# Sliding-window attention between two expert layers: one sigmoid per score block, and the blend ahead of the scores

## The reference

```python
x = x + 0.5 * ffn(layernorm(x))      # x W_base^T + b + gated low-rank experts (top 2 of 8)
x = x + attn(layernorm(x))
x = x + 0.5 * ffn(layernorm(x))      # the same weights

def attn(x):                         # H = 32 heads of DH = 128, one K and V for all heads
    Q, K, V = x @ Wq.T, x @ Wk.T, x @ Wv.T
    Qr, Kr = rope(Q), rope(K)
    for i in range(0, S, 256):       # windows of 512, half overlapping
        attn = sigmoid(Qr[i:i+512] @ Kr[i:i+512].T * SCALE)
        attn = attn / attn.sum(-1)
        wout = attn @ V[i:i+512]
        # first half: out = (1 - alpha) * out + alpha * wout; second half: out = wout
    return out @ Wo.T
```

## Time and profile before

| | |
|---|---|
| median of 3 executions | 4590.61 us (4590.13 to 4811.48) |
| the profiled execution, its own time | 4577.35 us |
| its span, slowest core (5) | 4575.8 us |
| spans of the eight cores | 4546.6 to 4575.8 us |
| mean granted TensorE clock of the cores | 0.826 to 0.832 |
| busy: TensorE, ScalarE, VectorE, GpSimd | 69%, 28%, 22%, 12% of the span |

### The profile page before, as it was taken

How to read it: one execution, slowest core, us unless ns; L and a number is a source line. 1 busy time by engine, 2 the same in 40 slices (tenths; PEclk the granted TensorE clock), 3 DMA queues, 4 the chain that set the end, 5 groups by cost and what they waited for, 6 DMA issues and landing times.

```text
span 4575.8 us, 40221 instructions; the slowest of 8 cores (4546.6 to 4575.8 us)
## 1 busy us (share of the span) xinstructions
PE 3136.4 (69%) x14804; PEld 1492.0 (33%) x14804; DVE 995.1 (22%) x1698; ACT 1303.2 (28%) x1727; POOL 533.3 (12%) x772
## 2 busy tenths in 40 slices
PE   2449999994366666666666666666676665349999
PEld 1224444442223332233332233322333321224444
DVE  3441111115612220012210023200122100441111
ACT  3332211214422322232322332223323232332222
POOL 1101111111111111200002100012000022101111
PEclk8669999996688777887778887778887787669999
DMA  5325565554453436831127711067411178427776
GB/s 126 97 58 166 169 178 171 171 152 119 124 150 111 124 97 117 145 88 37 56 44 143 145 37 46 28 112 141 97 37 50 36 140 155 110 79 209 221 223 188
DMA packets 647220, 537.35 MB, mean 117 GB/s; under 512 B 33905, under 2 KB 566642, under 8 KB 646770
## 3 DMA queue, kind: packets, MB, share of 16 engines
q0 software_dynamic: 90112, 251.71, 23.8%
q1 hardware_dynamic: 556914, 283.07, 23.3%
HBM read 408.85 MB, written 125.83 MB: 117 GB/s over the span
## 4 chain that ended last, share of the span: by engine, by line
PE 53%; DMA 18%; DVE 11%; ACT 10%; issue 5%; DVEq 1%; SPq 0%; ACTq 0%; POOL 0%; POOLq 0%
PE PS L441 24%; PE PS L754 7%; PE PS L602 7%; DMA x2h<-arena 6%; DMA arena<-wqT 4%; DMA arena<-woT 4%; PE PS L688 4%; ACT arena L273 4%; ACT arena L668 2%; PE PS L673 2%; DVE arena L248 2%; DVE arena L252 2%; DVE arena L695 2%; DVE arena L706 2%; PE PS L651 2%
## 5 line engine op out<-in xcount | busy, mean ns | idle before, releaser
L441 PE MATMUL PS<-arena 128*128 128x512 bf16 x5120 | 1135.7, 380 | 15.5 <-ACT arena L273 15.5
L273 ACT ACTIVATE arena<-arena 128x512 bf16<-128x512 f32 (+1 forms) x784 | 567.4, 762 | 1052.8 <-PE PS L444 578.3
L754 PE MATMUL PS<-arena 128*128 128x512 bf16 x2048 | 594.7, 456 | 348.9 <-ACT arena L273 348.9
L441 PEld LDWEIGHTS PS<-arena 128*128 128x128 bf16 x5120 | 501.9, 98 | 623.3 <-issue 22.3
L602 PE MATMUL PS<-arena 128*128 128x512 bf16 x2048 | 584.9, 428 | 19.7 <-ACT arena L273 19.6
L754 PEld LDWEIGHTS PS<-arena 128*128 128x128 bf16 x2048 | 222.8, 113 | 720.0 <-issue 582.9
L45 POOL DMA_DIRECT2D x2h<-arena x256 | 217.2, 849 | 1943.3 <-ACT arena L762 1683.7
L762 ACT ACTIVATE arena<-PS 128x512 f32<-128x512 f32 x256 | 152.8, 597 | 662.5 <-PE PS L754 448.9
L695 DVE COPY arena<-PS 128x516 f32<-128x516 f32 (+1 forms) x160 | 94.2, 589 | 1044.2 <-PE PS L688 1044.2
L602 PEld LDWEIGHTS PS<-arena 128*128 128x128 bf16 x2048 | 215.3, 108 | 264.7 <-issue 104.8
L448 DVE TENSOR_SCALAR arena<-arena 128x512 f32<-128x512 f32 x160 | 77.1, 482 | 823.2 <-DMA arena<-xin 464.6
(11 more groups left out here) (102 smaller groups left out, 2270.9 us busy)
## 6 DMA issues: line engine op xcount, KB each, us to landing
arena<-wbaseT SPq DMA_DIRECT2D x256, 512.0 KB, 6.7
x2h<-arena POOLq DMA_DIRECT2D x320, 256.0 KB, 4.7
arena<-wqT SPq DMA_DIRECT2D x256, 256.0 KB, 3.4
arena<-woT SPq DMA_DIRECT2D x256, 256.0 KB, 5.5
arena<-xin POOLq DMA_DIRECT2D x24, 1024.0 KB, 11.5
arena<-xin POOLq DMA_DIRECT2D x96, 256.0 KB, 5.3
x1h<-arena POOLq DMA_DIRECT2D x96, 256.0 KB, 2.4
arena<-x1h POOLq DMA_DIRECT2D x24, 1024.0 KB, 9.6
```

The costliest lines, as they stand in the source:

```text
L273: c = pr.emit("scalar", lambda s, si=i % nb, d=dst_bf_ap: s.activation(d, wstage[si], ACT.Copy), wc, 1)
L441: pr.emit("tensor", lambda t, c=c, sl=slot, of=of, t0=t0, n=n: t.matmul(sl, wb[of % 2][:, c, :], xlnb[:, c, t0:t0 + n], start=(c == 0), st ...
L754: mmc = pr.emit("tensor", lambda t, gg=gg, of=of, ts2=ts2, sl=slot: t.matmul(sl[:, 0:512], wqb[of % 2][:, gg, :], wout8[:, gg, ts2 * 512:( ...
```

## The change

In each window the blend, where one is pending, now comes first. Then each of the four key blocks has a matmul and a sigmoid of its own: blocks 0 and 2 in the first half of PS2, blocks 1 and 3 in the second. The matmul of block 2 waits for the sigmoid of block 0, that of block 3 for the sigmoid of block 1, and the first one for rope and the last sigmoid of the window before. `feed(6)` stands behind block 1 and behind block 3, `feed(4)` behind the matmuls with V as before; these wait for the sigmoid of block 3.

In `ln_prep` the index `par` of the float buffers `xf` and of their semaphores is renamed `xpar` (it is `i % 2` as before), the list of two buffers is written as a comprehension, and two semaphores `xload4` and `xload5` are declared. A list `sig_kc` is set up ahead of the heads. The rest of the diff:

```diff
@@ -637,12 +640,6 @@
                     npp = qn // 128
                     kc0 = wi * 2
                     sp = wi % 2
-                    w01 = [("vector", rope[h]), ("scalar", sig2_prev)]
-                    for kc in (0, 1):
-                        s01 = pr.emit("tensor", lambda t, kc=kc, q0w=q0w, qn=qn, kc0=kc0, par=par: t.matmul(
-                            PS2[:, kc * 512:kc * 512 + qn], krb[:, (kc0 + kc) * 128:(kc0 + kc + 1) * 128],
-                            qrb[par][:, q0w:q0w + qn], start=True, stop=True),
-                            w01 if kc == 0 else [], 1 if kc == 1 else 0)
                     if pend_blend is not None:
                         b, sA, wpar, dgc, hh_ = pend_blend
                         pend_blend = None
@@ -659,27 +656,31 @@
                         woutev = pr.emit("scalar", lambda s, hh_=hh_, b=b: s.activation(
                             wout8[:, hh_, b * 256:(b + 1) * 256], PS4[:, 0:256], ACT.Copy),
                             [("tensor", tw), ("tensor", womm_prev_grp)], 1)
+                    sgw = []
+                    if (h, wi - 2) in av_hist:
+                        sgw = [("tensor", av_hist[(h, wi - 2)])]
+                    elif wi < 2 and h >= 1:
+                        sgw = [("tensor", av_hist[(h - 1, 4 - wi)])]
+                    for kc in range(4):
+                        wsc = []
+                        if kc == 0:
+                            wsc = [("vector", rope[h]), ("scalar", sig_cnt)]
+                        elif kc >= 2:
+                            wsc = [("scalar", sig_kc[kc - 2])]
+                        smm = pr.emit("tensor", lambda t, kc=kc, q0w=q0w, qn=qn, kc0=kc0, par=par: t.matmul(
+                            PS2[:, (kc % 2) * 512:(kc % 2) * 512 + qn],
+                            krb[:, (kc0 + kc) * 128:(kc0 + kc + 1) * 128],
+                            qrb[par][:, q0w:q0w + qn], start=True, stop=True), wsc, 1)
+                        sig_kc[kc] = pr.emit("scalar", lambda s, qn=qn, sp=sp, kc=kc: s.activation(
+                            sgb[sp][:, kc, 0:qn],
+                            PS2[:, (kc % 2) * 512:(kc % 2) * 512 + qn],
+                            ACT.Sigmoid, scale=SCALE),
+                            [("tensor", smm)] + (sgw if kc == 0 else []), 1)
+                        if kc == 1:
+                            feed(6)
+                    sig_cnt = pr.cnt["scalar"]
+                    sig2_prev = sig_cnt
                     feed(6)
-                    wsg1 = [("tensor", s01)]
-                    if (h, wi - 2) in av_hist:
-                        wsg1.append(("tensor", av_hist[(h, wi - 2)]))
-                    elif wi < 2 and h >= 1:
-                        wsg1.append(("tensor", av_hist[(h - 1, 4 - wi)]))
-                    pr.emit("scalar", lambda s, qn=qn, sp=sp: s.activation(
-                        sgb[sp][:, 0:2, 0:qn], PS2[:].rearrange("p (c t) -> p c t", c=2)[:, :, 0:qn],
-                        ACT.Sigmoid, scale=SCALE), wsg1, 1)
-                    sig1 = pr.cnt["scalar"]
-                    for kc in (2, 3):
-                        s23 = pr.emit("tensor", lambda t, kc=kc, q0w=q0w, qn=qn, kc0=kc0, par=par: t.matmul(
-                            PS2[:, (kc - 2) * 512:(kc - 2) * 512 + qn],
-                            krb[:, (kc0 + kc) * 128:(kc0 + kc + 1) * 128],
-                            qrb[par][:, q0w:q0w + qn], start=True, stop=True),
-                            [("scalar", sig1)] if kc == 2 else [], 1 if kc == 3 else 0)
-                    feed(6)
-                    sig_cnt = pr.emit("scalar", lambda s, qn=qn, sp=sp: s.activation(
-                        sgb[sp][:, 2:4, 0:qn], PS2[:].rearrange("p (c t) -> p c t", c=2)[:, :, 0:qn],
-                        ACT.Sigmoid, scale=SCALE), [("tensor", s23)], 1)
-                    sig2_prev = sig_cnt
                     avm = 0
                     for p in range(npp):
                         for kc in range(4):
```

More of the change, by code:

```diff
@@ L25 @@
 STREAM_ENG = {"wload0": "sync", "wload1": "sync", "wload2": "sync", "wmisc": "sync",
-              "xload0": "gpsimd", "xload1": "gpsimd", "xload2": "gpsimd", "xload3": "gpsimd", "xstore": "gpsimd",
+              "xload0": "gpsimd", "xload1": "gpsimd", "xload2": "gpsimd",
+              "xload3": "gpsimd", "xload4": "gpsimd", "xload5": "gpsimd", "xstore": "gpsimd",
               "xsta": "gpsimd", "xstb": "gpsimd"}
@@ L185, in ln_prep @@
         a = Arena(arena_t, base)
-        xf = [a.f32(NIF * 128, (NIF, 128)), a.f32(NIF * 128, (NIF, 128))]
+        xf = [a.f32(NIF * 128, (NIF, 128)) for _ in range(2)]
         xb = [a.bf16(NIF * 256, (NIF, 256)), a.bf16(NIF * 256, (NIF, 256))]
@@ L195, in ln_prep @@
             par = i % 2
+            xpar = i % 2
             ps_st = [PSM[0:1, 0:256], PS1[0:1, 0:256]][par]
@@ L200, in ln_prep @@
             wld = wld + store_q()
[L201 to L204, removed]
+            sem = "xload%d" % xpar
+            semb = "xload%d" % (2 + xpar)
+            g0 = pr.dma(sem, xf[xpar][:, 0:16, :], src_r[:, 0:16, i * 128:(i + 1) * 128], wld)
+            g = pr.dma(semb, xf[xpar][:, 16:32, :], src_r[:, 16:32, i * 128:(i + 1) * 128], [])
             wsc = [(sem, g0)]
@@ L207, in ln_prep @@
                 wsc.append(("tensor", stats[i - 2]))
[L208 to L215, removed]
+            pr.emit("scalar", lambda s, p=par, xp=xpar: s.activation(
+                xb[p][:, 0:16, 0:128], xf[xp][:, 0:16, :], ACT.Copy), wsc, 1)
+            sh0 = pr.emit("scalar", lambda s, p=par, xp=xpar: s.activation(
+                xb[p][:, 0:16, 128:256], xf[xp][:, 0:16, :], ACT.Square), [], 1)
+            pr.emit("scalar", lambda s, p=par, xp=xpar: s.activation(
+                xb[p][:, 16:32, 0:128], xf[xp][:, 16:32, :], ACT.Copy), [(semb, g)], 1)
+            s1l[i] = s1 = pr.emit("scalar", lambda s, p=par, xp=xpar: s.activation(
+                xb[p][:, 16:32, 128:256], xf[xp][:, 16:32, :], ACT.Square), [], 1)
             wmm = [("scalar", sh0)]
@@ L566, in attn @@
         pend_blend = None
+        sig_kc = [0, 0, 0, 0]
         wq_sub = {}
```

8 lines of the change are left out of this document (4 added, 4 removed).

## The result

The changed kernel takes 0.9853 of the time before (95% interval 0.9811 to 0.9895): 1.5% less, some 68 us of 4600. Its profiled execution took 4541.9 us, with a span of 4540.4 on its slowest core (4), against 4577.35 and 4575.8. Both kernels have executions in which the cores of one die ran at a lower clock; the plain medians (4614.22 and 4600.12 us) hold them in different numbers, so only the ratio, which leaves them out, is used.

What follows compares the result with a forecast made beforehand. No engine is full: TensorE and VectorE's diagonals bound fed windows, latency unfed ones. Gains of 13.7 us (unfed heads) and 14 (fed heads) sum to 27.7, taking 4590.6 to 4563 us, range 4545 to 4588.

Steps and rivals of the forecast that it cites:

- Waits taken away: In heads, earlier sigmoids and V: 0.74 us per fed head (projection matmuls fill waits), 3.42 per unfed (no filling).
- step list: Fed window 2: worked-out start times from blend at 1371.99 to V at 1376.41, 0.10 us gained.
- my 3.42: Unfed head: gain in us over windows 0 to 4, 0.56 + 1.31 + 0.60 + 0.60 + 0.35.
- Unfed, 1.2 GHz: Windows 2 and 3 of unfed heads, worked out at half clock: V 0.60 us earlier in each.
- More than forecast: Denser unfed heads get the full clock, each saving another 7 us, 4535 us in all; chance 0.06.
- The discount of 20.7 to 14 us: Fed heads' summed gain of 20.7 us cut to 14, between all of it and about 7 lasting.
- the rival behind it: Fed heads: clock's rise doesn't come earlier, so earlier heads lose their lead; 4570 us, chance 0.20.
- The split's cost on ScalarE: 320 more activations: below 1 us extra occupancy per head, lying in ScalarE's idle time.
- The blend's place: Fed windows: blend ahead of the scores takes 0.43 us out of the wait's cover, onto TensorE's path.
- Nothing comes of it: Added waits and starts per window cost 26 us, nearly all the gain; 4575 to 4600 us, chance 0.15.
- Slower: Fed windows 2 and 3: clock falls in one 1.56 us wait before the blend; 4950 us, chance 0.03.
- The test named in advance: Seven fed heads 321 us, eighth head's stretch 3.4 less; wrong if mean clock moves over 0.01 from 0.80.

Runs made afterwards that it cites:

- e7: Kernel before plus useless matmuls in TensorE's waits at head ends, in window 0, window 4 and unfed windows; 0.9771 of the time before.
- e8: Changed kernel plus the same kind of useless matmuls, fewer where waits are shorter; attention 2358.5 us, against 2390.9 for the kernel before filled likewise.
- e10: Kernel before plus 13 useless matmuls in TensorE's waits in window 4 of the 28 fed heads; 0.9939 of the time before.
- e1: Kernel before with sigmoids split into four, blend left in its old place after the first two scores; attention 2434.0 us, against 2503.2 before.
- e2: Kernel before with only the blend put ahead of the scores, sigmoids still over pairs; 1.0006 of the time before.
- e4: Kernel before with only window 4 of the 28 fed heads in the changed form; 0.9991 of the time before.
- e5: Changed kernel's four sigmoids, but the blend behind all four scores and the second filling, right before V; 0.9484 of the time before.

## Why the prediction was wrong, and where it was right

**Waits taken away: right.** The fed window went as in the step list: V 4.42 us behind the blend's start, TensorE's one wait 1.57. At one clock (e7 against e8) the terms are 0.27 in w1 (0.2 in the sum), 0.11 and 0.10 in w2 and w3 (0.10 each), and 0.27 in w4 (0.26); the 0.08 of window 0 is not shown by that pair. An unfed head gave 2.49 at the full clock; my 3.42 was worked out for 1.2 GHz, where windows 0 and 1 gave 0.58 and 1.43 in the changed kernel for my 0.56 and 1.31. All waits together are 29 to 32 us, for my full sum of 34.4.

**The step that failed** is that the sums were made at the clock of before. I wrote of the unfed windows "Unfed, 1.2 GHz" and carried both sides of the comparison at that level, and took window 4 of a fed head at whatever clock its row had. But the clock of these windows was not fixed: in e10, where only TensorE's waits were filled, and in e1, e2 and e4, where its matmuls came closer together or into another order, V of window 4 was at full clock in 66 to 100% of fed heads instead of 6%. The change moves just that. Fed windows 4 gave 0.62 for 0.26, unfed windows 2 and 3 gave 0.92 and 1.58 for 0.60 each, and half clock in a fed head went from 19.7 to 15.8 us. I had this as the case "More than forecast", with a chance of 0.06 and only for unfed heads, where 4 x (5.20 - 2.49) = 11 of its 28 us came; the fed heads' part, 24 x (1.40 - 0.65) = 18, I had nowhere. The row from which I sized window 4 hid it: V at 1391.50 takes 0.62 us, the full clock, and belongs to the first head of a group. In the kernel before 94% of heads 2 to 7 had V at half clock there, as in the row of 1.03 us at 2120.82 above. The earlier trace rows show such heads, at half clock for more than 12 us behind the rope, but begin behind window 4.

**The discount of 20.7 to 14 us was wrong,** and so was the rival behind it. If a late rise of the clock held the heads at their length, neither the changed kernel's fed heads (46.47) nor e5's (40.28) could have become so much shorter than 47.87. Heads of 46.50 and 45.56 us follow one another, at clocks of 0.79 and 0.87: the clock's changes jump from head to head, and the head follows. The Trainium skill's rule (TensorE: Matmul & The Clock Gate, What's actually happening) that the monitor's window runs freely is not refuted by this; what was wrong is that I concluded from it that a lead is lost.

**The split's cost on ScalarE: right.** It is busy 20.5 us longer, hidden. By the figures of the Trainium skill, an estimate, it would have been some 30 (ScalarE: Activation LUTs, What ACT_TABLE_LOAD costs); the trace has less, and the trace decides. **The blend's place: right in sign and size** for the latency of fed windows (0.15 to 0.21 a window); that it also moves the clock, mostly for the better, I had not foreseen. **Nothing comes of it** fell: the added waits cost what was worked out. **Slower** came true only in a few places: behind the wait of 1.57 us the clock fell in 12 of the changed kernel's windows on eight cores (7 windows 2 of first heads, 5 windows 3 of fed ones), where the rival needed it in most.

**The test named in advance** said: seven fed heads in 321 us if the gain passes, wrong if the mean clock moves by more than 0.01. They took 319.11, and the clock moved by 0.02. By that last sign, which I had set myself, the account was wrong before any experiment ran. The stretch of the eighth head took 6.5 us less, for 3.4.

## What to carry to other kernels

Where TensorE waits often and briefly, price a change twice: once at the clock of the trace, and once with the question which matmuls it brings together or apart just ahead of the point where the clock falls. To find out which part is the clock, put matmuls of no use into the waits of both versions and compare them at one clock. And ask of each small block that waits for a slow engine what else could stand ahead of it: here moving the blend behind the scores was worth 175 to 227 us, the split 16 to 69. When such a step gives less in total than in its own stage, look for a wait that ends at a time which the step doesn't move, as the residual's copy does here.

## What the runs showed of the hardware

With matmuls that serve nothing, 13 in one window of a head, the granted clock stayed at 1.00 through the next 3 us and the head was 1.0 us shorter (e10); with some 60 in a head it stayed at 1.00 throughout (e7: half clock 0.0 us of 44.43). Two sigmoids of 512 columns, each behind a wait for its own matmul, took 1.08 us together where one takes 0.59: the wait of the second, already met, did not keep them from overlapping by 0.10.
